# Second layer of a fused recurrence: leak x h1 + gate x x1 as one scan of pairs on VectorE, GpSimd keeps only the output sum

## The reference, cut to what matters

```python
# layer 0, gated recurrence; its output is added to x
z = sigmoid(xzt + h @ U_z + vz)
r = sigmoid(xrt + h @ U_r + vr)
hh = tanh(xht + r * h @ U + vh)
h = (1 - z) * h + z * hh
# layer 1, leaky recurrence over x1 = x + h; it starts from h_t = cond_1024
leak = 1 - alpha
gate = sigmoid(h1 @ Wh.T + x1_t @ Wz.T + b)
h1 = tanh(h1 * leak + gate * x1_t)
# x2 = x1 + h1; layers 2 and 3 (gated cumulative sums, an adapted MLP) follow on all of x2
```

## Time and profile before

| | us |
|---|---|
| runs before | 1037.74, 1039.88, 1040.82; median 1039.88 |
| the profiled execution | 1039.51, its span 1037.7 |
| TensorE busy (matmuls) | 970.0 (93%) |
| VectorE busy | 789.4 (76%) |
| ScalarE busy | 622.4 (60%) |
| GpSimd busy | 256.3 (25%) |
| mean granted TensorE clock | 0.980 of full speed |

### The profile page before, as it was taken

How to read it: one execution, slowest core, us unless ns; L and a number is a source line. 1 busy time by engine, 2 the same in 40 slices (tenths; PEclk the granted TensorE clock), 3 DMA queues, 4 the chain that set the end, 5 groups by cost and what they waited for, 6 DMA issues and landing times.

```text
span 1037.7 us, 115126 instructions
## 1 busy us (share of the span) xinstructions
PE 970.0 (93%) x50964; PEld 807.0 (78%) x50964; DVE 789.4 (76%) x2496; ACT 622.4 (60%) x2795; POOL 256.3 (25%) x647
## 2 busy tenths in 40 slices
PE   5799999999999999999999998969999999999987
PEld 5699999999999999999999997436666655665655
DVE  2366767766667667766767675799999999999994
ACT  2577777777777777777777775324444444434440
POOL 0022222222222222222222222224223223222220
PEclk8899999999999999999999999979999999999999
DMA  5122321310100101101001001100001000001001
GB/s 208 51 82 68 104 81 57 108 32 25 33 23 25 33 25 27 31 23 35 23 25 33 25 23 32 26 1 24 23 23 45 23 23 23 23 23 41 27 23 41
DMA packets 38295, 42.02 MB, mean 40 GB/s; under 512 B 5120, under 2 KB 31232, under 8 KB 37120
## 3 DMA queue, kind: packets, MB, share of 16 engines
q1 hardware_dynamic: 36832, 40.55, 12.6%
q10 hardware_dynamic: 1440, 1.18, 0.4%
HBM read 32.80 MB, written 8.91 MB: 40 GB/s over the span
## 4 chain that ended last, share of the span: by engine, by line
PE 56%; DVE 31%; issue 8%; ACT 2%; DMA 1%; DVEq 1%; ACTq 0%; POOL 0%; POOLq 0%
PE bank L686 33%; PE bank L697 20%; DVE arena L613 10%; DVE wx L625 4%; DVE cx L629 4%; DVE cx L638 2%; DVE cx L642 2%; DVE none_h L555 2%; DVE wx L611 2%; DVE cx L634 2%; DVE y L653 2%; ACT cand_kept L373 1%; DMA bias<-in_bias 1%; PE bank L866 1%; PE bank L840 1%
## 5 line engine op out<-in xcount | busy, mean ns | idle before, releaser
L697 PE MATMUL bank<-x_ahead,wx 128*32 128x64 f32 x12376 | 291.1, 222 | 3.7 <-ACT bank L337 3.0
L686 PE MATMUL bank<-none_h,urz 128*32 128x32 f32 x16384 | 213.5, 200 | 21.3 <-DVE none_h L555 16.9
L697 PEld LDWEIGHTS bank<-x_ahead,wx 128*32 128x32 f32 x12376 | 220.5, 111 | 4.0 <-DMA x_ahead<-in_x 3.1
L686 PEld LDWEIGHTS bank<-none_h,urz 128*32 128x32 f32 x16384 | 191.7, 110 | 31.7 <-DVE none_h L555 25.2
L269 POOL TENSOR_TENSOR leaked<-leak,h_f 128x64 f32<-128x64 f32 x256 | 82.3, 321 | 487.0 <-ACT h_f L384 487.0
L543 DVE TENSOR_TENSOR rh_f<-r_f,none_h 128x32 f32<-128x32 f32 x512 | 112.9, 258 | 110.2 <-ACT r_f L364 110.2
L866 PE MATMUL bank<-x,wl 128*128 (+1 forms) x384 | 179.5, 607 | 0.9 <-DVE rank_rows L592 0.9
L424 ACT ACTIVATE arena<-bank,bl 128x512 f32<-128x512 f32 x96 | 66.0, 687 | 157.6 <-PE bank L866 157.6
L555 DVE TENSOR_TENSOR_SCAN none_h<-zero_z,cand_kept 128x64 f32<-128x64 f32 x512 | 121.4, 279 | 35.3 <-ACT cand_kept L373 17.6
L686 PE MATMUL bank<-rh_f,uh 128*32 128x32 f32 x8192 | 124.3, 199 | 11.2 <-DVE rh_f L543 3.5
L866 PEld LDWEIGHTS bank<-x,wl 128*128 128x128 f32 x384 | 71.5, 192 | 81.2 <-issue 79.7
(11 more groups left out here) (83 smaller groups left out, 1377.6 us busy)
## 6 DMA issues: line engine op xcount, KB each, us to landing
x_in<-in_x SPq DMA_DIRECT2D x34, 256.0 KB, 2.7
x_ahead<-in_x SPq DMA_DIRECT2D x130, 64.0 KB, 1.8
arena<-in_w SPq DMA_DIRECT2D x8, 1024.0 KB, 5.2
out<-y SPq DMA_DIRECT2D x32, 256.0 KB, 2.5
rank_rows<-in_bias_rows SPq DMA_DIRECT2D x1, 1024.0 KB, 4.9
arena<-scratch SPq DMA_DIRECT2D x64, 16.0 KB
cx<-in_cx SPq DMA_DIRECT2D x1, 768.0 KB, 4.4
wx<-in_wx SPq DMA_DIRECT2D x1, 768.0 KB, 7.3
```

Of the source, the lines that this page charges most:

```text
L686: mm = pe.matmul(out(m)[32 * j:32 * j + 32], weights(k, j, m), moving(k), start=False, stop=k == 1, tile_position=(0, 32 * j), skip_group_ ...
L697: mm = pe.matmul(out[32 * j:32 * j + 32], weights(k, j, m), moving(k), start=False, stop=False, tile_position=(0, 32 * j), skip_group_chec ...
```

## The change

The leak product moves into a scan. `h1_gx` holds pairs of h1 (written by the tanh) and gate x x1 (written by VectorE); `zero_leak` holds pairs of 0 and leak. With a = (0, leak) and b = (h1, gx) the scan gives first 0 x s + h1 = h1 and then leak x h1 + gx, which is the pre-activation. It lies in `h1_pre`, and the tanh reads every second element of it. The `leaked` product and its semaphore go, and GpSimd has one operation a step. In the last three steps, where VectorE's wait on `x2_done` in `first_output` is missing, ScalarE waits for it itself.

```diff
-        gx = sb("gx", [P, HALVES, B])
-        leaked = sb("leaked", [P, 2, HALVES, B])
-        pre1 = sb("pre1", [P, 2, HALVES, B])
-        h1_f = sb("h1_f", [P, 2, HALVES, B])
+        zero_leak = sb("zero_leak", [P, HALVES, B, 2])
+        h1_gx = sb("h1_gx", [P, 2, HALVES, B, 2])
+        h1_pre = sb("h1_pre", [P, 2, HALVES, B, 2])
...
-            pool.wait_ge(leak_done, 1)
-            pool.wait_ge(first_in, 16 * len(FIRST_LOADS))
-            pool.tensor_tensor(leaked[:, 0], leak[:], cond_f[:], ALU.mult).then_inc(leaked_done, 1)
             def turn(n):
                 for u in range(BODY):
                     s = n * BODY + u
                     pool.wait_ge(h1_done, 2 * (s + 2 + LAG))
-                    pool.tensor_tensor(leaked[:, (u + 1) % 2], leak[:], h1_f[:, u % 2],
-                                       ALU.mult).then_inc(leaked_done, 1)
-                    pool.tensor_tensor(x2[:, :, :, s], x1_f[:, u % LOOP], h1_f[:, u % 2],
+                    pool.tensor_tensor(x2[:, :, :, s], x1_f[:, u % LOOP], h1_gx[:, u % 2, :, :, 0],
                                        ALU.add).then_inc(x2_done, 1)
...
-                act.activation(h1_f[:, at], pre1[:, at], ACT.Tanh).then_inc(h1_done, 2)
+                act.activation(h1_gx[:, at, :, :, 0], h1_pre[:, at, :, :, 1], ACT.Tanh).then_inc(h1_done, 2)
...
             for u in range(LAG):
                 second_gate(TURNS, u)
+                act.wait_ge(x2_done, T - LAG + u)
                 second_state(TURNS, u)
...
-            dve.memset(h1_f[:, 0], 0.0)
+            dve.memset(h1_gx[:, 0], 0.0)
+            dve.memset(zero_leak[:], 0.0).then_inc(leak_zero, 1)
             dve.wait_ge(alpha_in, 32)
             dve.memset(eps[:], EPS).then_inc(eps_done, 1)
-            dve.tensor_scalar(leak[:], leak[:], -1.0, 1.0, ALU.mult, ALU.add).then_inc(leak_done, 1)
+            dve.wait_ge(leak_zero, 1)
+            dve.tensor_scalar(zero_leak[:, :, :, 1], leak[:], -1.0, 1.0, ALU.mult, ALU.add).then_inc(leak_done, 1)
...
-            dve.tensor_copy(h1_f[:, 1], cond_f[:]).then_inc(h1_done, 2 * (1 + LAG))
+            dve.tensor_copy(h1_gx[:, 1, :, :, 0], cond_f[:]).then_inc(h1_done, 2 * (1 + LAG))
...
                 dve.wait_ge(gate_done, s + 1)
-                dve.tensor_tensor(gx[:], gate_f[:], x1_f[:, (u - LAG) % LOOP], ALU.mult).then_inc(gx_done, 1)
+                dve.tensor_tensor(h1_gx[:, (u - LAG - 1) % 2, :, :, 1], gate_f[:], x1_f[:, (u - LAG) % LOOP], ALU.mult).then_inc(gx_done, 1)
...
                 dve.wait_ge(gx_done, s + 1)
-                dve.wait_ge(leaked_done, s + 1)
-                dve.tensor_tensor(pre1[:, at], gx[:], leaked[:, at], ALU.add).then_inc(pre1_done, 1)
+                flat = lambda w: w.rearrange("p h b a -> p (h b a)")
+                dve.tensor_tensor_scan(flat(h1_pre[:, at]), flat(zero_leak[:]), flat(h1_gx[:, 1 - at]),
+                                       0.0, ALU.mult, ALU.add).then_inc(pre1_done, 1)
...
-                      lambda k: h1_f[:, (s - 1) % 2, k]).then_inc(gate_pre, 1)
+                      lambda k: h1_gx[:, (s - 1) % 2, k, :, 0]).then_inc(gate_pre, 1)
```

More of the change, by code:

```diff
@@ L137, in build_program @@
         alpha_in, hidden_in = sem("alpha_in"), sem("hidden_in")
-        leak_done = sem("leak_done")
+        leak_zero, leak_done = sem("leak_zero"), sem("leak_done")
         r_pre, z_pre, cand_pre, gate_pre = sem("r_pre"), sem("z_pre"), sem("cand_pre"), sem("gate_pre")
@@ L143, in build_program @@
             sem("zero_done"), sem("rh_done"), sem("kept_done"), sem("h_done"), sem("x1_done"))
-        gx_done, pre1_done, leaked_done, x2_done = (
-            sem("gx_done"), sem("pre1_done"), sem("leaked_done"), sem("x2_done"))
+        gx_done, pre1_done, x2_done = (
+            sem("gx_done"), sem("pre1_done"), sem("x2_done"))
         ln_step, std_done, ada_done, hid_pre, hid_done = (
```

## The result

The changed kernel takes 1051.24 us (median of 4 runs, 1049.87 to 1051.63) against 1038.81 (1035.76 to 1040.82) before; the ratio is 1.012, with a 95% interval of 1.0091 to 1.0148. That is 12.4 us slower, where 27 were forecast. The time lies inside the range of 1047 to 1074, but the size was off by a factor of two, and rival B (1056) was nearer than A (1067).

What follows compares the result with a forecast made beforehand. TensorE's own instructions were taken to pace the recurrence. Stalls of 0.48 us a cycle less 0.05 for today's collisions, times 63 cycles, gave 27.1 us; with 0.2 more, 1039.5 became 1067 us, range 1047 to 1074.

Steps and rivals of the forecast that it cites:

- rival B: At the shared port VectorE's reset product goes first; only wh's stall costs, 0.25 us a cycle, 1056 us; chance 0.30.
- A: At the shared port GpSimd's sum goes first, holding the first reset product: 0.43 us a cycle net, 1067 us; chance 0.50.
- the scan's price: On VectorE, the 128-element scan replacing the 0.20 us add takes 0.41 us, so the pre-activation is 0.21 us later.
- VectorE and x1 have room: VectorE's x1 starts at most 0.21 us later with 0.29 free before the next reset product: zero cost.
- the late tanh pushes the reset gates: On ScalarE, a tanh 0.21 us later delays the reset gate at u=2 by 0.15 to 0.21, less at u=1 and u=3.
- the idle time that was to show it: Loads of wh at u = 1, 2 and 3 should show idle time that h1's tanh ends; none at u = 0.
- GpSimd's saving: GpSimd's busy time falls by 82 us without the leak product, with no effect of its own.
- the second starts right behind the tanh: h1's end + 0.07: On GpSimd, the sum, without the leak product ahead, starts 0.07 us after the tanh ends, upon the first reset product.
- later stalls don't absorb earlier ones: they add to 0.37 us a cycle: On TensorE at wh, h1's delay less slack costs 0.10 (u=3), 0.12 (u=1) and 0.15 us (u=2), summed per cycle.
- The rule of the lock: At the port VectorE and GpSimd share, whichever instruction starts first holds it throughout and the other blocks; GpSimd would mostly win.
- D: Rival: not slower, the scan costs no more than h1's slack and fewer collisions save 3 us, 1036 us; chance 0.04.
- E: Rival: nothing moves, since the real slack at TensorE's loads is larger than the margins show, 1040 us; chance 0.06.

Runs made afterwards that it cites:

- e6: The kernel before without GpSimd's leak product in the loop, the add reading a constant tile: 1037.01 us, ratio 0.999.
- e12: The changed kernel with GpSimd's sum writing to a fixed column, so its address needs no register work: 1068.25 us, ratio 1.0244.
- e4: The changed kernel with the loop's wh product reading a constant tile of zeros and not waiting for h1: 1050.13 us, ratio 1.0087.
- e5: The changed kernel with GpSimd's sum waiting for both reset products and the wh product reading a constant tile without waiting for h1: 1033.41 us, ratio 0.9955.
- e11: The changed kernel with GpSimd's sum waiting for both reset products and the tanh moved behind the next step's reset gates: 1088.72 us, ratio 1.0434.
- e2: The changed kernel with GpSimd's sum also waiting for both reset products of the step: 1035.63 us, ratio 0.9946.
- e1: The changed kernel with GpSimd still running a leak product, which nobody reads, ahead of its sum: 1074.17 us, ratio 1.0311.
- e9: The changed kernel with GpSimd's sum waiting for VectorE's next product (L542) too: 1053.12 us, ratio 1.0141.

## Why the prediction was right in sign and wrong in size

**Right:** the scan's price (0.40 us against 0.41) and the tanh's (0.01), that h1 is late by 0.21, that the added time is all in the recurrence, that VectorE and x1 have room, that the steps u = 1, 2 and 3 wait at `wh` and u = 0 does not (but for the idle time that was to show it), that the late tanh pushes the reset gates, that GpSimd's saving has no effect of its own (e6), and that VectorE's products and GpSimd's sum collide where the time goes.

**Wrong, first: "the second starts right behind the tanh: h1's end + 0.07".** This step chose A over B. The 0.07 was read from the leak product, the first of two instructions, and carried to the sum, which was always second; its address could be computed while the product ran. With the product gone, the register work stands behind the wait: 0.16 us measured, 0.08 in e12, where it isn't needed. That puts the sum 0.05 behind the start of the first reset product and not 0.04 ahead. The mechanism of A was right, at the start that it assumed: e12's cycle is 0.35 us over that of before, where 0.43 were reckoned.

**Wrong, second: "later stalls don't absorb earlier ones: they add to 0.37 us a cycle"**, and with it B's 0.25. A wait at `wh` isn't carried to `uh`, because TensorE runs the loads behind it faster (0.32 and 0.37 us from `wh` to `uh` against 0.37 and 0.47). Why it does is not shown; that its register instructions run during the wait is a guess. e4 and e5 show that the stall at `wh` costs nothing at this size, and e11 that a longer one does. The profiled executions differ by 10.3 us: 0.145 us in each of the 57 cycles is 8.3, and 2.2 stand ahead of them. The other 2 of the 12.4 us are spread between runs. e2 gives back all of it and more by the sum's place alone. B's 1056 came near by luck: its price was that of `wh`, while the measured one is the second product's, which B had as covered.

**The rule of the lock.** What the prediction cites from the Trainium skill ("SBUF — State Buffer", section "SBUF: two separate sides"), that one of two instructions is blocked until the other is through, was borne out by e1, e12 and e9. That the first to start wins holds for the recorded starts in e1 (0.03 us apart) and e12 (0.04), where GpSimd was ahead, and in the changed kernel, where the product was ahead by 0.05. It does not hold for a product queued right behind another: in the kernel before, the sum at u=2 starts 0.01 us ahead of the second product in each of the 57 cycles and holds it in 17. Perhaps the recorded start of a queued instruction isn't its request; no run shows that.

**The rivals.** D was excluded by the scan's length and rightly so, for the loss; but a version with the scan at its full price can be faster than before (e2), which no rival had. E held for the half of the mechanism that I had rested on: at `wh` the margins were not the whole of what TensorE can take, since it makes up part of a wait.

## What to carry to other kernels

Two engines that share a port need a place for each other's work, not less work: moving one instruction took the changed kernel from 1.2% over the one before to 0.5% under it, by one wait on a semaphore that was there already. A collision that costs next to nothing today can cost more after a change elsewhere: the products were held before as long as after, and it took the 0.21 us of the scan to put the hold where TensorE waits for it. When an instruction ahead of another is removed, look at what the second did under its cover (address, registers), for its start moves by that. And a margin between a result and its use isn't the slack of an engine with a queue: take the wait out, or make it longer, and see whether the time follows.

## What the runs showed that was not expected

In e12 GpSimd clears x2 before the loop, in two instructions of 7 us that read nothing. VectorE's `tensor_scalar` (a single SBUF input) and the transpose that follows hung on them for almost 9 us each, against 0.19 and 0.44 otherwise:

```profile
6.21 8.82 DVE L492 TENSOR_SCALAR zero_leak<-leak 128x64 f32<-128x64 f32 x1 [4.11 <-issue]
...
6.32 8.72 DVE L493 STREAM_TRANSPOSE bias_f<-bias_rows 128x256 f32<-128x256 f32 x1
...
8.06 6.92 POOL L258 MEMSET x<- 128x8192 f32 x1
```

Both end at 15.03 and 15.04, 0.05 after the second clear (14.98). The loop starts 6.3 us later for it (25.9 against 19.6). And TensorE's 32 loads of `wh` take 0.42 us in a queue without pauses and 0.35 behind a wait, which is part of why waits of up to about 0.1 us were free there.
